# A fused four-layer graph network: attention's row sums inverted and its probabilities scaled on VectorE instead of GpSimd

## The reference, cut to what matters

```python
x = _layernorm(x + _L0_gnn_ref(x, adj, ...), axis=-1)   # masked gram matrix, rows normalized, times values
x = _layernorm(x + _L1_gnn_ref(x, adj, ...), axis=-1)   # normalized adjacency times x W, plus bias
x = _layernorm(x + _L2_gnn_ref(x, adj, adj, ...), axis=-1)   # three steps of a gated recurrent unit
x = _layernorm(x + _L3_gnn_ref(x, adj, ...), axis=-1)   # attention, 8 heads of 32

# in _L3_gnn_ref:
scores = jnp.einsum('bqhd,bkhd->bhqk', q, k) / jnp.sqrt(jnp.float32(HD))
scores = scores + (1.0 - adj)[None, None, :, :] * -1000000000.0
attn = jax.nn.softmax(scores, axis=-1)
out = jnp.einsum('bhqk,bkhd->bqhd', attn, v).reshape(b, n, d)
return out @ Wo + bo
```

## Time and profile before

| what | us |
|---|---|
| median of three runs | 2265.41 (2263.5 to 2267.77) |
| the profiled execution | 2266.11 |
| its span in the trace | 2264.3 |
| PE busy | 2079.4 |
| DVE busy | 1582.8 |
| ACT busy | 1259.3 |
| POOL busy | 972.9 |

### The profile page before, as it was taken

The page is one execution under the profiler, slowest core; times in us unless marked ns, Lnnn a source line. Parts: engine busy times, 40 slices in busy tenths (PEclk is TensorE's granted clock), DMA queues, the critical chain, the costliest instruction groups (busy, mean ns, idle before and its releaser), DMA issues.

```text
span 2264.3 us, 34780 instructions
## 1 busy us (share of the span) xinstructions
PE 2079.4 (92%) x12342; PEld 1658.8 (73%) x12342; DVE 1582.8 (70%) x3423; ACT 1259.3 (56%) x2516; POOL 972.9 (43%) x1138
## 2 busy tenths in 40 slices
PE   5779999999999999999999999999999999999966
PEld 4667777777777777777777777777777777778743
DVE  5556677677767767776776777677776777777742
ACT  3225646466564656646465564646556465665644
POOL 3013434445354444534444353444435344454534
PEclk8889999999999999999999999999999999999987
DMA  4002021130211203011120211112020111202030
GB/s 125 1 19 60 16 57 47 31 73 20 49 36 50 54 22 75 26 38 47 38 66 20 66 38 39 47 38 66 20 66 27 50 47 38 66 20 66 20 77 27
DMA packets 65616, 101.16 MB, mean 45 GB/s; under 512 B 11424, under 2 KB 31136, under 8 KB 65440
## 3 DMA queue, kind: packets, MB, share of 16 engines
q1 hardware_dynamic: 65440, 98.87, 17.2%
HBM read 23.34 MB, written 8.39 MB: 14 GB/s over the span
## 4 chain that ended last, share of the span: by engine, by line
PE 70%; DVE 17%; ACT 7%; issue 4%; POOL 1%; DMA 1%; SPq 0%; DVEq 0%; POOLq 0%; ACTq 0%
PE ps L850 15%; PE ps L852 15%; PE ps L851 15%; PE ps L872 10%; PE ps L958 5%; PE ps L942 5%; DVE fa L828 4%; DVE fa L826 3%; DVE xn L649 3%; ACT pT L394 2%; PE ps L972 2%; DVE fa L829 2%; ACT fa L533 1%; PE ps L1185 1%; PE ps L1056 1%
## 5 line engine op out<-in xcount | busy, mean ns | idle before, releaser
L677 DVE CUSTOM_DVE_ANT_0 fa<-ps,mask 128x512 f32<-128x512 f32 x512 | 332.4, 687 | 263.5 <-PE ps L942 263.3
L302 POOL TENSOR_TENSOR rsum<-esum,mhalf 128x2 f32<-128x2 f32 x256 | 199.6, 780 | 713.3 <-ACT fa L399 713.3
L308 POOL TENSOR_SCALAR fa<-fa,rsum 128x512 f32<-128x512 f32 x512 | 411.5, 816 | 53.0 <-POOL rsum L302 53.0
L394 ACT COPY pT<-ps 128x512 f32<-128x512 f32 x512 | 296.0, 583 | 195.5 <-PE ps L958 195.4
L399 ACT ACTIVATE fa<-fa,nmax 128x512 f32<-128x512 f32 x512 | 366.5, 723 | 53.7 <-DVE nmax L677 52.3
L958 PE MATMUL ps<-ident,fa 128*128 128x128 f32 x2048 | 311.1, 279 | 40.1 <-ACT pT L394 31.3
L958 PEld LDWEIGHTS ps<-ident,fa 128*128 128x128 f32 x2048 | 246.1, 143 | 126.5 <-ACT pT L394 40.5
L872 PE MATMUL ps<-adjT,ra 128*128 128x512 f32 x1024 | 260.7, 404 | 21.6 <-DVE ra L772 11.9
L664 DVE TENSOR_TENSOR ra<-ps,ra 128x512 fp32r<-128x512 f32 x224 | 151.1, 687 | 183.2 <-ACT ra L497 99.2
L872 PEld LDWEIGHTS ps<-adjT,ra 128*128 128x128 f32 x1024 | 191.8, 191 | 77.5 <-DVE ra L772 22.9
L942 PE MATMUL ps<-ra 128*128 128x512 f32 x512 | 178.8, 430 | 6.3 <-DMA ra<-ra 4.7
(11 more groups left out here) (183 smaller groups left out, 4682.6 us busy)
## 6 DMA issues: line engine op xcount, KB each, us to landing
ra<-ra SPq DMA_DIRECT2D x512, 128.0 KB, 2.4
fa<-in_x_T SPq DMA_DIRECT2D x17, 512.0 KB, 4.7
fa<-in_x SPq DMA_DIRECT2D x17, 512.0 KB, 3.9
out<-fa SPq DMA_DIRECT2D x16, 512.0 KB, 3.1
fa<-in_L_gnn_w_w SPq DMA_DIRECT2D x3, 512.0 KB, 8.6
adj_n<-in_adj SPq DMA_DIRECT2D x1, 1024.0 KB, 5.8
fa<-in_L_gnn_u_w SPq DMA_DIRECT2D x2, 256.0 KB, 9.1
fa<-in_L_gnn_Wk SPq DMA_DIRECT2D x1, 256.0 KB, 5.8
```

The costliest lines, as they stand in the source:

```text
L302: nc.gpsimd.tensor_tensor(rsum[:, 2 * k:2 * k + 2], esum[:, 2 * k:2 * k + 2], mhalf[:, 4:6], ALU.pow).then_inc(rs_r, 1)
L308: nc.gpsimd.tensor_scalar(SC[:, g], SC[:, g], rsum[:, 2 * k + u:2 * k + u + 1], 1.0, ALU.mult, ALU.mult).then_inc(nrm, 1)
L394: copy(pT[:, k % SLOTS, half(c)], ps[:, pt_bank(k, c), :].rearrange("p (a b) -> p a b", a=2)).then_inc(pt_c, 1)
L677: nc.vector.tensor_tensor_reduce(out=SC[:, s % RING], in0=ps[:, 4 + u], in1=mask[:, 2 * (k % 8 // 4) + u], scale=-1.0, scalar=3.0e38, op0= ...
```

## The change

`probabilities` leaves POOL. A function `scaled(b, k)` on DVE does the same work: it waits for the exponentials, inverts two columns with a reciprocal, waits for that, and multiplies the two tiles in place by a column each. `masked(k)` calls `scaled(t, k-1)` at its end for k from 2 to 15. Chunk 15 is scaled in the next pass, behind the first low part of the head, and chunk 0 between the statistics of layer 1 and their normalization. On POOL the four additions for X4 and `xT_lo` now stand in one row behind `rstd_of(3, o)`.

```diff
-            def probabilities(b, k):
-                gp.wait_ge(ex, b * TILES + (2 * k + 2))
-                nc.gpsimd.tensor_tensor(rsum[:, 2 * k:2 * k + 2], esum[:, 2 * k:2 * k + 2], mhalf[:, 4:6],
-                                        ALU.pow).then_inc(rs_r, 1)
-                gp.wait_ge(rs_r, b * CHUNKS + (k + 1))
-                settle(gp, "pool")
-                for u in range(2):
-                    g = (2 * k + u) % RING
-                    nc.gpsimd.tensor_scalar(SC[:, g], SC[:, g], rsum[:, 2 * k + u:2 * k + u + 1], 1.0,
-                                            ALU.mult, ALU.mult).then_inc(nrm, 1)
...
@@ def masked(k), on DVE
+                    if k > 1:
+                        scaled(t, k - 1)
+
+
+                def scaled(b, k):
+                    dve.wait_ge(ex, b * TILES + (2 * k + 2))
+                    nc.vector.reciprocal(rsum[:, 2 * k:2 * k + 2], esum[:, 2 * k:2 * k + 2]).then_inc(rs_r, 1)
+                    dve.wait_ge(rs_r, b * CHUNKS + (k + 1))
+                    for s in (2 * k, 2 * k + 1):
+                        TS(SC[:, s % RING], SC[:, s % RING], rsum[:, s:s + 1], None, ALU.mult).then_inc(nrm, 1)
...
                 if i is not None:
                     tile_lo(AB0, 2, 0, y_h, i * 2 + 1, y_l)
+                if o is not None:
+                    scaled(o, 15)
...
                     sums_and_statistics(1, o1_ps, dinv, xg)
+                if t is not None:
+                    scaled(t, 0)
                 if i is not None:
                     normalize(xg, xg, 1, 0, i, x2_r)
```

More of the change, by code:

```diff
@@ L176, in gnn_stack @@
         sc_ps = sem("score_ps"); ttr = sem("score_masked"); ex = sem("score_exp"); nrm = sem("prob_ready")
-        rs_r = sem("row_sum_inverted")
+        rs_r = sem("row_sum_inverted_by_dve")
         pt_ps = sem("probT_ps"); pt_c = sem("probT_copied")
@@ L321, in body @@
             def body(i, t, o):
-                if o is not None:
-                    probabilities(o, 15)
                 if t is not None:
@@ L333, in body @@
                     add_row(xg, b1row, xb_r)
-                if t is not None:
-                    probabilities(t, 0)
                 if i is not None:
                     rstd_of(1, i)
-                if t is not None:
-                    for k in range(1, 6):
-                        probabilities(t, k)
                 if o is not None:
@@ L343, in body @@
                 if t is not None:
-                    for k in range(6, 15):
-                        if k >= 10 and k < 10 + NT:
+                    for k in range(10, 10 + NT):
+                        if k < 10 + NT:
                             if k == 10:
```

## The result

| | before | after |
|---|---|---|
| median, us | 2265.42 (2263.5 to 2267.77) | 2391.56 (2388.78 to 2394.28) |
| span of the profiled execution | 2264.3 | 2387.0 |
| PE busy | 2079.4 | 2114.0 |
| DVE busy | 1582.8 | 1801.6 |
| ACT busy | 1259.3 | 1267.1 |

The changed kernel takes 1.0556 times the time before (95% interval 1.0538 to 1.0575), 126 us more. The forecast was 2386, with a range from 2315 to 2435: it was right. A full pass went from 133.2 us to 141.2 (medians). The profiled execution is the fastest of the four (2388.78 us, mean granted clock 0.971 against 0.967 to 0.969 in the others), so the trace explains 122.7 of the 126 us.

The account below looks back on a forecast made before the run. PE was taken to bound the 15 full passes; 7.8 us a pass made 117, less 1 for the first pass, plus 8 for the clock, less 3 for the last pass: 121 us more, 2386 us, range 2315 to 2435.

Parts of the forecast that it names:

- S: DVE's time for one `scaled`, a reciprocal and two multiplies: 1.0 us, between 0.9 and 1.1.
- full-rate rival: Multiply by a column on DVE runs at 1.05 ns an element, S is 1.4 us, time 2428 us; chance 0.13.
- The five waits at places without slack: PE waits longer a pass: head 1.0 us, layer norm 1.9, step 0's low part, chunk 2 and chunk 3 1.0 each.
- `xT_lo`: End of step 2: chunk 13's multiplies on DVE meet this POOL instruction, making the h stage 1.5 us late a pass.
- shared bandwidth: Alternative rule for DVE beside GpSimd: the `xT_lo` term would be about nil, the sum 22 us less.
- The h stages: End of each step: S more work less DVE's 0.2 us wait and the 0.7 us given back, net +0.1 us.
- relief: h stages: instructions no longer stretched by POOL's scalings give back 0.7 us a step.
- the seven places where S counts: Head, norm, three in step 0, two further h stages; at full rate each grows 0.4 us, 42 us over 15 passes.
- The clock: PE idle at the layer norm brings half-clock stretches, 1.7 us lost each, in a third of passes: about 8 us.
- The last attention pass: Pass without i, a latency chain: scaling on DVE shortens it, -3 us, between -12 and +5.
- Amount: Follow-up experiments' rival: only the total put on DVE counts, 0.49 us for each of 256 scalings wherever it stands.
- slack: Delays in a pass partly overlap; head and `xT_lo` at nil, step 0 half: 2327 us; chance 0.22.

Follow-up runs that it names:

- the half-size run: Changed kernel with VectorE multiplying only the first 256 of 512 columns of each tile, the rest left unscaled: 2342.06 us, 1.0333.
- the split of x: Kernel before, with GpSimd's split of the next x in the head waiting until VectorE has normalized x3: 2238.43 us, 0.9879.

## Why the prediction was right, and where not

**S.** Taken as 0.19 + 2 x 0.41; measured 0.19 from reciprocal to multiply and 0.80 to what follows: 0.99. The duration of a tile was taken as 0.49 and is 0.485. The step that found it, the bound from line 649's longest case, holds: the half-size run gives 0.52 ns an element. These are the two rows of the kernel before on which it rests; the multiply ends at 963.72, the GpSimd instruction at 963.58, and all 15 full passes have such a pair with 0.14 to 0.15 us between the ends.

```profile
961.16 2.56 DVE L649 TENSOR_SCALAR xn<-xn,mv,rstd 128x256 f32<-128x256 f32 x1
961.18 2.40 POOL L292 TENSOR_TENSOR ra<-fa,ra 128x1024 fp32r<-128x1024 f32 x1
```

The Trainium skill's table of rates ("VectorE: DVE Perf Modes", "The perf-mode tier table") has such an instruction at twice the rate, and the durations of line 670 (485 ns, and 353 ns at half the size) now show it with a column as its operand; the full-rate rival falls.

**The five waits at places without slack** (head, norm, three in step 0) were predicted at 5.9 us and measured at 6.2 with the clock, 5.9 without; each was taken back by a run, the three of step 0 in one run, whose trace shows three separate gains. The reasoning that worked was to take the one instruction that PE waits for with no time between, and count what comes ahead of it in DVE's list.

**`xT_lo`** was predicted at 1.5 us and measured at 1.4, and the run that cuts it shows the cause. The Trainium skill's rule ("SBUF — State Buffer", "Who interferes with whom"), that such a Vector instruction and a GpSimd one exclude each other, agrees: one multiply in each of 15 passes takes 2.60 us, and ends 0.3 us behind a POOL instruction of 2.38. By shared bandwidth the prediction put the term at about nil.

**The h stages.** The net of about 0.1 a step was right (0.0 to 0.2), and so was the relief: 0.7 a step predicted and 0.7 measured by moving GpSimd's multiplies aside. Its source was named too narrowly: taking the multiplies away alone gave 0.56 a step, since an X4 addition stretches the h stage of step 1 as well. In the kernel before, 15 of line 829's 30 stretched cases stand beside such an addition and not beside a scaling. What was wrong is in the full-rate rival: "the seven places where S counts" are eleven. At S = 1.4 the pass would have grown by 11 x 0.4 = 4.4 us, so that rival's time should have been 2386 + 66 = 2452, outside the range. The prediction had the pieces (S less wait and relief) and did not ask what happens to their difference when S grows.

**The clock.** Predicted 8 us, from falls of 1.7 us each in a third of the passes; measured some 8 us, 5.5 in the 14 passes and 2.7 behind them. The place was right: eight falls begin right behind the norm's waits, and the run that takes chunk 0's scaling off DVE has none there (its five are in step 2, but for one). That the size came out is luck, two errors in opposite directions: falls are twice as frequent (11 in 14 passes), and one of 3.4 us at the norm costs 0.1 to 0.9 us (the pass less its counterpart before, above the 7.7 of passes without a fall) and not 1.7. In step 2 a fall does cost 1.4 to 1.7 us, as four passes of the run with chunk 0 on GpSimd show, and the two near the end cost 1.3 and 1.4. The difference fits what PE waits for: after the norm it soon waits for the gather, 1.10 us in the rows above, and what it does slower ahead of a wait is not lost. That reason is argued from the rows. Why the same wait brings a fall in some runs and passes more than in others (with chunk 15 on GpSimd 2 of 14 passes have one at the norm, with `xT_lo` cut 12) stays open.

**The last attention pass.** Predicted -3 (between -12 and +5); measured +0.6 against the kernel before. The failed step is "a chunk's way falls from 2.4 on POOL to about 1.1 on DVE, but it must stand behind the next mask": the second half of that sentence, which got no number, takes back the first. The size is small against the 121. Added up for the profiled execution: 115.0 for the places (117 - 1 predicted), 8.2 for the clock (8) and 0.6 for the last attention (-3), less 1.0 ahead of the first full pass that belongs to no term, make 122.8 against the 122.7 between the spans.

**Amount and slack.** The "slack" rival (2327) supposed that delays overlap within a pass. They don't: the single gains, taken back one by one, add up to the whole (-7.9 of 8.1).

## What to carry to other kernels

An engine with 27% idle time has no room at a point where another engine takes its result with no time between: count, for each added instruction, the first such result behind it in the list, up to the next wait that would absorb it. Offloading a busy-looking engine that nobody waits for (GpSimd, 43% busy, 6.9 us of waits) gains only what its work does to its neighbours, and that can be had by moving a few instructions in time (2.6% here, of which the split of x is 1.2) without loading the engine on whose results PE waits. Price a fall of the clock by its place: one of 3.4 us cost 1.3 to 1.7 us in step 2 and at the end, but 0.1 to 0.9 us where PE had to wait soon after. When a small term is the difference of two large ones, keep both for the rivals.

## What the runs showed of the hardware

- A multiply of 128 x 512 float32 by one column in SBUF takes VectorE 485 ns, of 128 x 256 353 ns: 0.22 us fixed and 0.52 ns an element. Two in a row cost 0.40 each from start to start.
- Beside a GpSimd instruction of 128 x 1024 (2.38 us) it takes up to 2606 ns, beside one of the 128 x 256 additions (0.78 us) 0.96 us (9 cases in full passes). GpSimd's inversions of 128 x 2 delay it not at all: the pair at 1186.43 took its 0.88 us beside one, which itself took 0.94 instead of 0.71 (15 cases).
- A two-source instruction of 128 x 512 (the h stage) takes 0.98 to 1.10 us instead of 0.69 beside a GpSimd scaling or addition of some 0.7 us, 0.3 to 0.4 us more. That happens in 45 of 96 cases on line 828 and 30 of 96 on line 829; their means of 853 and 814 ns hide it. A one-source multiply loses the whole of the GpSimd instruction. Moving the multiplies to VectorE exchanged the first kind of meeting for the second.
